# Attention with relative positions and a routed expert layer: operands in pairs of buffers, score rows loaded for each pass, bias operands in quarters, 64-column near products, no pauses on TensorE

## What is computed

```python
xn = layernorm(x)
q, k, v = split(xn @ w_qkv.T)          # 4 batches x 16 heads = 64 (batch, head) pairs, N = 1024, hd = 8
attn = q k^T + take(q @ rpe_k_table, bucket(j - i)) + take(k * scale @ rpe_q_table, bucket(j - i))^T
attn = softmax(attn)                   # bucket(d) = clip(d, -31, 31) + 31, 63 buckets
out = attn @ v + (attn summed by bucket) @ rpe_v_table
x = x + out @ w_proj.T + b_proj + routed_experts(xn) + shared_expert(xn)
```

## Time and profile before

| what | us |
|---|---|
| median of 3 runs | 1528.76 |
| lowest, highest of them | 1524.4, 1531.94 |
| span of the profiled execution, first to last instruction | 1522.0 |
| PE busy, PEld busy | 1325.6, 895.9 |
| DVE busy, ACT busy, POOL busy | 1111.2, 797.9, 541.3 |

### The profile page before, as it was taken

How to read it: one execution, slowest core, us unless ns; L and a number is a source line. 1 busy time by engine, 2 the same in 40 slices (tenths; PEclk the granted TensorE clock), 3 DMA queues, 4 the chain that set the end, 5 groups by cost and what they waited for, 6 DMA issues and landing times. The chain is left out here.

```text
span 1522.0 us, 75140 instructions
## 1 busy us (share of the span) xinstructions
PE 1325.6 (87%) x32698; PEld 895.9 (59%) x32698; DVE 1111.2 (73%) x2461; ACT 797.9 (52%) x1408; POOL 541.3 (36%) x552
## 2 busy tenths in 40 slices
PE   2785399999999999988989899999999999999887
PEld 1352256666666666655668565666666666666555
DVE  7684378888888888887764676777777767777762
ACT  1332135655665666655541455665666555656544
POOL 3453212222222222222434244444444444444423
PEclk9897559999999999999995799999999999999999
DMA  4444546666556555554564566666666666666532
GB/s 97 138 142 138 159 158 200 200 207 193 186 183 191 190 176 183 181 184 153 174 189 145 160 183 182 183 192 198 186 183 196 183 176 180 190 183 183 149 104 58
DMA packets 167209, 260.10 MB, mean 171 GB/s; under 512 B 33980, under 2 KB 89397, under 8 KB 166886
## 3 DMA queue, kind: packets, MB, share of 16 engines
q1 hardware_dynamic: 155414, 248.46, 52.5%
q0 software_dynamic: 11472, 6.83, 3.7%
HBM read 145.14 MB, written 112.37 MB: 169 GB/s over the span
## 5 line engine op out<-in xcount | busy, mean ns | idle before, releaser
L1408 DVE TRANSPOSE_TENSOR_REDUCE tops<-PS 128x16 f32<-128x512 f32 x1024 | 689.7, 699 | 190.1 <-PE PS L697 183.9
L1096 ACT ACTIVATE PT<-PS 128x512 f32<-128x512 f32 x1024 | 590.2, 596 | 423.4 <-PE PS L697 416.1
L697 PE MATMUL PS<-Qs,Ks 73*32 73x512 bf16 (+29 forms) x11904 | 666.4, 322 | 66.8 <-DVE tops L1408 45.6
L697 PEld LDWEIGHTS PS<-Qs,Ks 73*32 73x32 bf16 (+1 forms) x11904 | 308.9, 97 | 266.7 <-DVE tops L1408 94.0
L697 PE MATMUL PS<-PT,Vst 128*9 128x256 f32 (+7 forms) x7552 | 345.4, 286 | 12.6 <-issue 12.1
L638 POOL COPY WP<-PT 128x768 f32<-128x768 f32 x128 | 105.3, 822 | 645.4 <-ACT PT L1096 460.9
L697 PE MATMUL PS<-WT,eye 96*32 96x96 bf16 (+2 forms) x4352 | 294.7, 206 | 0.2 <-issue 0.2
L697 PEld LDWEIGHTS PS<-PT,Vst 128*9 128x9 f32 x7552 | 187.8, 91 | 82.6 <-issue 32.3
L697 PEld LDWEIGHTS PS<-WT,eye 96*32 96x32 bf16 x4352 | 186.8, 99 | 22.5 <-issue 1.2
L657 POOL TENSOR_TENSOR ajp<-dq_s,ajp 128x508 bf16<-128x508 f32 x128 | 147.3, 1151 | 10.4
L626 POOL DMA_INDIRECT acc_d<-XNA,tok_i x64 | 100.8, 1575 | 78.8 <-DMA acc_d<-XNA,tok_i 66.2
(11 more groups left out here) (199 smaller groups left out, 1025.9 us busy)
## 6 DMA issues: line engine op xcount, KB each, us to landing
aj_d<-ajp SPq DMA_DIRECT2D x64, 768.0 KB
WT<-aj_d SPq DMA_DIRECT2D x192, 256.0 KB
dq_d<-dq_e SPq DMA_DIRECT2D x64, 512.0 KB, 5.3
dq_s<-dq_d SPq DMA_DIRECT2D x64, 512.0 KB, 3.9
TOE<-toe_d SPq DMA_DIRECT2D x33, 768.0 KB, 5.8
q_stack<-PT SPq DMA_DIRECT2D x24, 256.0 KB, 2.5
Qs<-q_stack SPq DMA_DIRECT2D x64, 96.0 KB
Ks<-k_stack SPq DMA_DIRECT2D x64, 96.0 KB
```

What stands on the lines that cost most here:

```text
L697: return pe.matmul(o, l, r, start=start, stop=stop, skip_group_check=True)
L1096: act.activation(PT[:, TILE + N * J + 512 * half:TILE + N * J + 512 * half + 512], PS[:, 2 + u % 2, :], ACT.Exp).then_inc(s2_read, 1)
L1408: dve.tensor_reduce(tops[:, (h + 1) % 2, s // 2, 16 * (s % 2):16 * (s % 2) + 16], PS[:, s % 2, :].rearrange("p (c i) -> p c i", i=TILE), A ...
```

## The change

What it does, part by part:

- **Rows for each pass.** The rings `Qs` and `Ks` of five heads become four buffers of two heads: `Q1`, `K1` for the first pass, `Q2`, `K2` for the second. SP loads a head's rows for each pass (`load_rows`, five transfers, called twice), and once more for `dq` (`Qd` and `tabq`, `load_dq`) and for `aj` (`Ka` and `tabk`, `load_aj`). The zero rows are set once, so `zero_d` goes.
- **Bias operands in quarters.** `WT` holds two heads, not three, and each head's three parts are loaded in four pieces of two key blocks (`load_windows(t, q)`), at four places of SP's iteration, each with its waits. `aj_d` has three heads.
- **Near products.** 24 products of 64 columns in two column groups, the edges' eight alternating between them. `Ym` is 512 wide, not 256, half of it masked away.
- **No pauses**, and TensorE's program is called with a plain h.
- **Waits.** POOL's `window` waits for `pv_done`, not for `s2_read`. DVE drains where it waited for its own semaphores (two places per head), and waits for `s2_ready` where it waited for `mrow_in`. The store of `dq_d` waits for `aj_psum`, not for `dq_in`.

```diff
-        aj_d = dram("aj_d", [2, 3, P, N], BF16)
+        aj_d = dram("aj_d", [3, 3, P, N], BF16)
-        Qs = sb("Qs", [ROWS, RING, N], BF16)
-        Ks = sb("Ks", [ROWS, RING, N], BF16)
-        tab = sb("tab", [ROWS, RING, 2, P], BF16)
-        WT = sb("WT", [P, 3, 2 * N])
+        Q1 = sb("Q1", [ROWS, PAIR, N], BF16)
...
+        Qd = sb("Qd", [ROWS, N], BF16)
+        Ka = sb("Ka", [ROWS, N], BF16)
+        tabq = sb("tabq", [ROWS, P], BF16)
+        tabk = sb("tabk", [ROWS, P], BF16)
+        WT = sb("WT", [P, PAIR, 2 * N])
...
+            def load_rows(h, Qx, Kx, rows_in):
+                (b, hh), r = place(h), h % PAIR
+                tok = slice(b * N, b * N + N)
+                sp.dma_start(Qx[0:48, r, :], q_stack[hh * HD:hh * HD + HD, :, tok].rearrange("d n t -> (d n) t")).then_inc(rows_in, 16)
+                sp.dma_start(Kx[0:48, r, :], k_stack[hh * HD:hh * HD + HD, :, tok].rearrange("d n t -> (d n) t")).then_inc(rows_in, 16)
+                sp.dma_start(Qx[ROW_M + 6:ROW_M + 12, r, :], q_far[hh, :, tok]).then_inc(rows_in, 16)
+                for m, row in ((0, ROW_M + 3), (1, ROW_M + 12)):
+                    sp.dma_start(Kx[row:row + 3, r, :], k_far[hh, 3 * m:3 * m + 3, tok]).then_inc(rows_in, 16)
...
+            def load_windows(t, q):
+                sp.wait_ge(aj_out, 16 * (t + 1))
+                wait(sp, s2_ready, SLOTS * (t - 2) + 4 * q + 4)
...
+                for part in range(3):
+                    sp.dma_start(WTb[TILE * part:TILE * part + TILE, t % PAIR, :, 2 * q:2 * q + 2, :].rearrange("p s j n -> p s (j n)"),
+                                 shear(t % 3, part, 2 * q, 2)).then_inc(wt_in[q], 16)
...
                     sp.dma_start(dq_s[:, :], rows(dq_d, 1, [[DROW + 1, P], [1, N]])).then_inc(dq_in, 16)
+                if on(4):
+                    wait(sp, dq_psum, h + 4)
+                    load_dq(h + 4)
+                load_windows(h + 1, 2)
                 if on(0):
                     sp.wait_ge(mparts_ready, h + 1)
...
+                if on(2):
+                    if h + 1 >= 0:
+                        sp.wait_ge(s1_ready, SLOTS * (h + 1) + 1)
+                    load_rows(h + 2, Q1, K1, rows1_in)
+                load_windows(h + 1, 3)
                 if on(4):
-                    wait(sp, s2_ready, SLOTS * h)
-                    load_queries(h + 4)
-                if on(2):
...
+                    wait(sp, aj_psum, 2 * (h + 4))
+                    load_aj(h + 4)
+                if on(1):
+                    if h >= 0:
+                        sp.wait_ge(s2_ready, SLOTS * h + 1)
+                    load_rows(h + 1, Q2, K2, rows2_in)
...
+                load_windows(h + 2, 0)
                 if on(3):
                     t = h + 3
                     sp.wait_ge(aj_parts, 2 * t + 2)
...
                 if on(4):
                     sp.wait_ge(dq_copied, h + 5)
-                    wait(sp, dq_in, 16 * (h + 4))
+                    wait(sp, aj_psum, 2 * (h + 4))
                     sp.dma_start(dq_d[:, 64:64 + N], dq_e[:, :]).then_inc(dq_out, 16)
+                load_windows(h + 2, 1)
...
-                pool.wait_ge(s2_read, SLOTS * h + 8 * part + 8)
+                pool.wait_ge(pv_done, NJ * h + 4 * part + 4)
...
-            pause(START)
...
-                for b, k in [(8 + 8 * q + a, 0) for a in range(8) for q in range(4)] + [(b, -1) for b in range(8)] + [(b, 1) for b in range(40, 48)]:
+                edges = [x for b in range(4) for x in ((b, -1), (20 + b, 1))]
+                for b, k in [(4 + 8 * g + a, 0) for a in range(8) for g in range(2)] + edges:
+                    g, a = divmod((b - 4) % 16, 8)
...
-                pause(9)
...
-                        dve.wait_ge(s1_read, SLOTS * h + SLOTS)
+                        dve.drain()
...
-                        dve.tensor_tensor(Ym[:, :].rearrange("p (t a x) -> p a t x", t=NJ, x=4),
-                                          PS[:, 6, 0:256].rearrange("p (a t x) -> p a t x", t=NJ, x=4),
+                        dve.tensor_tensor(Ym[:, :].rearrange("p (m x) -> p m x", x=8),
+                                          PS[:, 6, :].rearrange("p (m x) -> p m x", x=8),
```

More of the change, by code:

```diff
@@ L790, in bias, with own, scores @@
                 return ins
-            def scores(bank, half, J, r, r3):
+            def own(sem_, value, per):
+                wait(pe, sem_, value)
+            def scores(bank, half, J, r, Qx, Kx):
                 pieces = []
@@ L836, in values @@
-                    wait(pe, o_copied, h - 1)
-                own = []
+                    own(v_ready, h + 1, 1)
+                    own(o_copied, h - 1, 1)
+                parts = []
                 for q in range(4):
@@ L845, in values @@
                         t = e
-                    own.append(mine)
+                    parts.append(mine)
                 PTJ = PT[:, TILE + N * J:TILE + N * J + N].rearrange("p (t q x) -> p t q x", q=4, x=TILE)
-                for n in range(max(map(len, own))):
-                    for mine in own:
+                for n in range(max(map(len, parts))):
+                    for mine in parts:
                         if n < len(mine):
@@ L879, in columns_of @@
                     ins.then_inc(pj_T, 1)
-                pe.wait_ge(on_ready, heads)
-                pe.wait_ge(s2_read, SLOTS * HEADS)
+                own(on_ready, heads, 1)
+                own(s2_read, SLOTS * HEADS, SLOTS)
                 columns_of(groups[0])
@@ L979, in _ @@
-            steps = iterations(pe, iteration)
-            next(steps)
+                        values(h - 1, (s - LAG - 3 + SLOTS) // 2)
+            for h in range(-4, 2):
+                iteration(h)
+            for h in range(2, hm):
+                iteration(h)
             pe.wait_ge(dq_copied, hm + 4)
-            pe.wait_ge(s1_read, SLOTS * (hm + 1))
-            pe.wait_ge(s2_read, SLOTS * hm - LAG)
+            own(s1_read, SLOTS * (hm + 1), SLOTS)
+            own(s2_read, SLOTS * hm - LAG, SLOTS)
@@ L1027, in _ @@
             pe.wait_ge(ex_yc, QUADS)
-            for _ in steps:
-                pass
+            for h in range(hm, HEADS + 2):
+                iteration(h)
             project(projected(None, None), HEADS)
```

254 lines of the change are left out of this document (123 added, 131 removed).

## The result

| | before | after |
|---|---|---|
| median of 4 runs each | 1530.34 us (1524.40 to 1531.94) | 1717.38 us (1709.53 to 1724.66) |
| ratio, 95% interval | | 1.123 (1.118 to 1.128) |
| profiled execution, span | 1528.76, 1522.0 us | 1724.66, 1722.9 us |
| mean granted clock | 0.937 | 0.852 |

The change costs 187 us. The direction was forecast, the size was not: 1613 us, with a range up to 1690.

A forecast was written before the change was run, and what follows sets the result against it. TensorE bound most of a head; SP's in-order list would take over: 60 heads at 20.5 us, three at 19.3, plus 14 us, 1302 against 1218.3, so 1528.8 + 84 = 1613 us, range 1535 to 1690.

The forecast's parts named there:

- first mechanism: SP's in-order issue list grows by 16 issues a head, to 32, and its cycle makes TensorE wait: +84 us.
- signs named for it: SP's `dq_d` and POOL waits shrink, `dq_s` waits exceed 60 us, TensorE under 85% busy, `top` 20 to 21 us apart.
- the clock rival: TensorE idles 1 to 3 us every head and its clock falls: 22.5 us a head, 1733 us; chance 0.14.
- SP's cycle, 20.5 us: SP's time per head after the change, against 19.3 before: list, landing of `dq_d` and overlong issues; 60 heads pass at it.
- 12.8 us of list: SP's issues from `dq_s` to the next `dq_d`: loads, window pieces, maxima rows and `aj_d`, at plain issue times.
- long issues: SP issues lasting 0.6 to 1.0 us too long; 3.6 a head at 0.9 us, 2.4 us of it in the cycle.
- the extra issues of the first half: 31 issues on SP (`acc_d`, `xn_d`, weight loads) that used idle time and now lie in the cycle: 14 us.
- from the ends above: Range of SP's cycle, 19.6 to 21.9 us, from bounds on window-piece cost and overlong issues (18.1 to 22.1): 1560 to 1697 us.
- Pauses at nothing: Removing TensorE's 1449 pauses of 51 ns, 74 us if unhidden, changes nothing: its queue, then SP's cycle, covers them.
- Near products, 0.3 us a head gained: TensorE's near block gets 0.3 us a head shorter, but inside its new idle time, so zero in the total.
- The break-even rival: SP's cycle is 18.5 to 19.4 us, overlong issues being rare: 1521 to 1536 us; chance 0.08.
- The reading on record: SP's overlong issues are held up while instructions are fetched, about four packets of 16.4 KB a head; stated as not shown.

The follow-up runs named there:

- a_whole: Kernel after with 32-column near products, pauses restoring 1024 instructions a head, and windows loaded whole in 3 issues into a ring of three: 1584.65 us, ratio 1.032.
- b_win12: Kernel before with the same window bytes, at the same place and under the same waits, loaded by 12 issues instead of 3: 1662.34 us, ratio 1.090.
- a_paced_fill: Kernel after with 32-column near products, pauses, and 7 unread 512-column products before TensorE's `dq_s` wait replacing 14 pauses (two in a few heads): 1675.93 us, ratio 1.104.
- a_fill: Kernel after with 30 small products a head, whose output nothing reads, ahead of TensorE's wait for `dq_s`: 1668.47 us, ratio 1.090.
- a_paced: Kernel after with the 32-column near products of before and pauses, so a head is again 1024 TensorE instructions: 1699.97 us, ratio 1.109.
- b_start0: Kernel before without the 58 pauses at the start of TensorE's program, nothing else changed: 1781.68 us, ratio 1.163.
- b_dup8: Kernel before with 8 more SP issues a head behind the window loads, 2 KB DRAM copies that nothing waits for: 1680.84 us, ratio 1.096.

## Why the prediction missed

*Direction and first mechanism: right.* SP's list becomes what TensorE waits for. a_whole (nine issues fewer, 115 us back) and b_win12 (nine more, 137 us lost) show it from both sides, and most signs named for it are there: the waits for `dq_d` and POOL shrink, `dq_s` waits grow to 104.9 us, TensorE's share is 83%. But `top` steps are 23.6 us apart, not 20 to 21, and the granted clock over the heads is below 0.9, which was the sign of the clock rival.

*SP's cycle, 20.5 us: short by 0.9 at a full clock, by 2 in fact.* The sum had 12.8 us of list and 2.4 of long issues, 15.2; a_paced_fill has 13.7 issuing and 1.3 of spaces, 15.0, though with more in the long ones (4.0 over the whole cycle) and less in the plain ones. `dq_d` to `dq_s` was put at 5.3 and is 5.7. The window pieces that stand there do not cause this: SP idles about 1.5 us behind them before it issues `dq_s`, as the forecast had it, and a_whole, without them, has 5.8. No idle time was left in the list; 0.9 us are there. That is 21.6, 1.1 more than forecast; 0.2 of it are the extra issues of the first half, which the forecast added apart (14 us), so 0.9 a head or some 54 us over 60 heads. The piece of `WT`, at 0.43 us, was right (0.432). Where the forecast took its range from cycles of 19.6 to 21.9 us "from the ends above", its own upper end was 22.1, which makes 1709 us.

*The clock: the step that failed.* "At the low level the waits that bring it vanish" was the reason to give that rival 0.14 and to keep it apart from the forecast. They do not vanish. TensorE's low clock makes SP wait (2.9 us in the list, 1.2 when a_fill keeps the clock up), SP's next `dq_s` is late again, and 412 us pass at the low level where it was 84. The two are one case, not rivals: SP's cycle brings the clock down, and the clock lengthens SP's cycle. Fillers take this out. Of the 104 us that were missed, a_fill gives back 49; the 55 by which it still exceeds the forecast agree with the 54 of the cycle. On a_paced, fillers give 24 us by the medians, not clear of the noise. The rival's own time, 1733 us, is near the measured one by luck: it had most heads at the low level, where 412 of some 1400 us are. The earlier trace rows had shown how it begins: 1.91 us of waiting, then 0.57. The Trainium skill (TensorE: Matmul & The Clock Gate, Why this matters for your kernels) warns of idle gaps between bursts, and the runs agree: 2.99 us for `dq_s` brought 20.4 us at 0.50, and 2.63 us in b_start0 a mean of 0.67 over 10 us.

*Pauses at nothing: wrong.* "TensorE's queue of issued products covers them" treats them as a cost. They are the opposite: they hold the instruction packets ahead of the stores, which is worth 80 us in the kernel before. In the changed kernel the error hides: pauses and the old near products together give 17 us there, not clear of the noise.

*Near products, 0.3 us a head gained: wrong.* 1.61 us at full clock where 1.66 was, and 2.8 at half. *`Ym`*: 692 ns, 0.27 more, within the 0.43 given, and covered.

*The break-even rival* leaned on long issues being rare. They rose from 1.2 to 3.1 us a cycle. The reading on record, that an instruction packet holds them up, fits the kernel before: from 190 us on 119 issues last more than 0.4 us above the shortest of their kind, and every one of them overlaps an instruction packet (TensorE's or the other instruction queue's), where of the 978 others 198 do; the median ends 0.39 us after the packet. In the kernel after it fits only a part: 73 of 208 overlap none, and 71 of these are pieces of `WT` issued between `dq_d` and `dq_s`, 1 us a cycle, which fall into the landing wait. What holds those was not looked for, and that a packet holds the others was not tried by itself.

*Left open.* a_whole is still 55 us above the kernel before, with seven issues more in each head, the rows loaded twice, pairs in place of rings of five, and its waits. Its cycle is 0.9 us longer, which over the heads is this amount; which of these parts makes it so was not tried.

## What to carry to other kernels

Where one queue issues everything in order, count its whole cycle, issue times, spaces and the landing it waits for, and do not spend its mean idle time: about half of the issue time that was added here arrived in the time although SP had idled 5.8 us a head. Where a program is long and fully unrolled, its own instruction packets are a transfer with a due time; look where they fall against the largest stores, and after every edit of the instruction count look again, or a part that got shorter reads as a loss (33 us here). And when a wait of 2 to 3 us appears on TensorE, look for a stretch at half clock behind it and add it, with what that makes late in turn.

## What was not expected of the hardware

- TensorE stands for want of instructions: 2.0 to 4.1 us a time in b_start0, when a 16.4 KB packet is asked for while 1280 KB of stores are in the DMA queues; it then starts some 4 us late (5.3 us behind the issue of `aj_d` where it was 0.3, with 1 us of it the shift itself). Moving all packets by 58 instructions was worth 252 us of 1530. The Trainium skill (Runtime: NRT & Kernel Launch, Instruction fetch mechanics) calls the cost of crossing a block "mostly hidden"; it is in the kernel before, where one of 254 packets from 240 us on starts at a count over 440, and not where a store burst is ahead of the packet.
- Stretches at the low clock lasted from 3.4 to 23.9 us in the heads. In b_start0 behind 1000 us one came in almost every head, in the kernel after long ones in every second head from 1240 to 1340 us.
- A copy of 2 KB within DRAM took SP 0.59 us to issue (b_dup8), longer than a load of 96 KB (0.46).
- Matmuls of TensorE that only keep it busy made the changed kernel faster by 49 us (a_fill).
